# Row factors of a four-layer graph network: spread over the partitions by DMA instead of by TensorE

## What is computed

```
x = layernorm(x + L0(x, adj))      # attention, 4 heads of 32
x = layernorm(x + L1(x, adj))      # GAT, 1 head
x = layernorm(x + L2(x, adj))      # GAT, 8 heads of 16
x = layernorm(x + L3(x, adj))      # MLP, GAT of width 256 without mask, MLP, GAT of width 128
# a GAT:  e = leaky_relu(s1[:, None] + s2[None, :], 0.2), masked by adj
#         out = softmax(e, axis=-1) @ h
```

## Time and profile before

| | |
|---|---|
| median of 3 runs | 1170.52 us (1170.07 to 1173.26) |
| the profiled execution | 1170.96 us, its span 1169.1 us |
| mean granted TensorE clock | 0.976 |
| busy, PE / DVE / ACT / POOL | 1057.2 / 924.0 / 740.8 / 260.1 us |
| DMA | 12.97 MB, 9490 packets |

### The profile page before, as it was taken

How to read it: one execution, slowest core, us unless ns; L and a number is a source line. 1 busy time by engine, 2 the same in 40 slices (tenths; PEclk the granted TensorE clock), 3 DMA queues, 4 the chain that set the end, 5 groups by cost and what they waited for, 6 DMA issues and landing times. The chain is left out here.

```text
span 1169.1 us, 26405 instructions
## 1 busy us (share of the span) xinstructions
PE 1057.2 (90%) x9333; PEld 778.1 (67%) x9333; DVE 924.0 (79%) x2514; ACT 740.8 (63%) x1901; POOL 260.1 (22%) x381
## 2 busy tenths in 40 slices
PE   2898999999999999999999999999999999889763
PEld 1566667868676776768677776767677767476342
DVE  4458898898898988888897888888898897877432
ACT  1788577767666776777676666677676765343432
POOL 0011212222222122222213122222213122230211
PEclk9999999999999999999999999999999999899876
DMA  3000000000000000000000000000000000000000
GB/s 117 2 10 11 10 2 11 1 10 2 19 2 20 1 20 1 11 10 2 19 2 20 1 12 9 11 10 2 20 1 11 1 11 6 5 10 1 10 9 10
DMA packets 9490, 12.97 MB, mean 11 GB/s; under 512 B 2705, under 2 KB 5009, under 8 KB 9233
## 3 DMA queue, kind: packets, MB, share of 16 engines
q1 hardware_dynamic: 9360, 11.28, 3.0%
HBM read 7.08 MB, written 4.19 MB: 10 GB/s over the span
## 5 line engine op out<-in xcount | busy, mean ns | idle before, releaser
L1119 DVE SCALAR_TENSOR_TENSOR P<-bank,t2e,mask_t 128x512 f32<-128x512 f32 x512 | 347.4, 740 | 22.7 <-PE bank L561 22.7
L941 DVE CUSTOM_DVE_ANT_0 probs<-bank,mask_add 128x512 f32<-128x512 f32 x256 | 171.3, 679 | 26.0 <-PE bank L462 25.5
L703 ACT ACTIVATE probs<-probs,neg_max 128x512 f32<-128x512 f32 x256 | 183.0, 717 | 13.2 <-DVE neg_max L949 13.1
L713 ACT ACTIVATE probs_t<-bank 128x512 f32<-128x512 f32 x256 | 148.3, 598 | 56.6 <-PE bank L470 55.8
L470 PE MATMUL bank<-ident,probs 128*128 128x128 f32 x1024 | 143.9, 276 | 10.7 <-ACT probs L703 6.6
L470 PEld LDWEIGHTS bank<-ident,probs 128*128 128x128 f32 x1024 | 113.8, 141 | 34.0 <-issue 16.1
L612 PE MATMUL bank<-t,l_P 128*128 128x257 f32 x512 | 125.2, 392 | 9.4 <-DVE l_P L1051 9.3
L571 PE MATMUL bank<-P,GH 128*32 128x512 f32 x1024 | 120.6, 613 | 10.4 <-issue 5.2
L612 PEld LDWEIGHTS bank<-t,l_P 128*128 128x128 f32 x512 | 95.0, 194 | 36.5 <-DVE l_P L1051 17.2
L748 ACT ACTIVATE x<-x,shift_l,rstd_l 128x128 f32<-128x128 f32 x256 | 104.1, 486 | 16.3 <-POOL shift_l L1252 16.1
L571 PEld LDWEIGHTS bank<-P,GH 128*32 128x32 f32 x1024 | 31.3, 112 | 84.0 <-issue 76.5
(11 more groups left out here) (161 smaller groups left out, 1914.7 us busy)
## 6 DMA issues: line engine op xcount, KB each, us to landing
x_in<-in_x SPq DMA_DIRECT2D x16, 256.0 KB, 2.7
out<-x SPq DMA_DIRECT2D x16, 256.0 KB, 2.0
l_P<-in_adj SPq DMA_DIRECT2D x1, 1024.0 KB, 5.0
w_fc<-in_L_gnn_W_fc SPq DMA_DIRECT2D x1, 256.0 KB, 3.0
probs_t<-in_L_gnn_a_fc SPq DMA_DIRECT2D x1, 256.0 KB, 5.8
w_cat<-in_L_gnn_W SPq DMA_DIRECT2D x2, 64.0 KB, 2.8
w3a<-in_L_gnn_mlp_w SPq DMA_DIRECT2D x1, 128.0 KB, 3.1
w3b<-in_L_gnn_mlp_w SPq DMA_DIRECT2D x1, 128.0 KB, 2.9
```

Of the source, the lines that this page charges most:

```text
L703: act.activation(e, e, ACT.Exp, bias=neg_max[:, m:m + 1], scale=SCALE0, accum_out=g.of(den0)[:, m:m + 1])\
L713: act.activation(probs_t[c % 2][:, h, :, :].rearrange("p j n -> p (j n)"), ps("l0_t", g, m)[:, :], ACT.Copy)\
L941: dve.tensor_tensor_reduce(probs[c % 2][:, h, :], ps("l0_s", g, m)[:, :], mask_add[:, c, :], 1.0, -3.0e38, ALU.add, ALU.max, row_max[:, m: ...
L1119: last = dve.scalar_tensor_tensor(P2[:, h % GROUP2, j, :], ps("l2_s", g, h)[:, :], g.of(t2e)[:, j, h:h + 1], mask_t[:, j, :], ALU.max, ALU ...
```

## The change

The transposes l1_s, l3_s, l3b_s, l2_s and the products l0_rd go, with their uses of PSUM banks. Instead SP moves the factors. For each of them a first DMA (`*_rows`) writes the tile [128, heads, 4] to a line in DRAM, [heads, 128 p, 4 c], in pieces of 16 bytes. Once it has landed, a second DMA per head (`*_spread`; four of 32 partitions each in layer 0) reads the 2 KB line and writes it to all 128 partitions of one of seven row buffers [128, 128 p, 4 c]. Before it reuses a row buffer, SP waits until VectorE has read it. Per graph these are 5 writes to DRAM and 15 spreading DMAs (12 x 256 KB in all).

The row buffer holds the factors in the order (p, c), since the line does. VectorE reads it with a rearranged view, "q p c -> q c p": 128 elements with a step of four float32 words, four times. All its other operands stay as they were. P, the mask and the output keep their order.

On POOL the large instructions over [128, 4 x 128] are cut in pieces of 128 columns: `l0_bias`, `l1_y`, `scale`, `l2_scale` and `below_zero` issue 4 (8 for layer 3's 1024 columns) where they issued 1. All five order tables and the bank table are new.

```diff
-            def l2_s(g, h):
-                if h == 0:
-                    pe.wait_ge(*sig("exp2", g, 3))
-                ps = empty("l2_s", g, h)
-                for c in range(C):
-                    last = pe.transpose(ps[:, c * P:(c + 1) * P], g.of(R2)[:, h, c:c + 1].broadcast_to([P, P]), ident[:, :])
-                last.then_inc(filled("l2_s", g, h), 1)
...
+            def lay_out(n, column, made):
+                def f(g, k):
+                    sp.wait_ge(*made(g))
+                    if n == "l0" and g.has(2):
+                        sp.wait_ge(*sig("o0_made", g, 1, back=2))
+                    sp.dma_start(g.of(line[n]).rearrange("h p c -> p h c"), column(g)).then_inc(signal[n + "_rows"], 16)
+                return f
+
+            def free_row(stage, g, k):
+                r, _, last = row_use[stage, k, g.i]
+                if last:
+                    sp.wait_ge(*row_read(last[0], last[2], last[1]))
+                return rows[r], row_filled[r]
+
+            def spread(n):
+                def f(g, k):
+                    if k == 0:
+                        sp.wait_ge(*sig(n + "_rows", g, 16))
+                    to, done = free_row(n + "_spread", g, k)
+                    sp.dma_start(to[:, :, :].rearrange("q p c -> q (p c)"),
+                                 g.of(line[n])[k].rearrange("p c -> (p c)").rearrange("(o n) -> o n", o=1)
+                                 .broadcast_to([P, N_NODES])).then_inc(done, 16)
+                return f
...
             def l2_p(g, h):
-                dve.wait_ge(*wrote("l2_s", g, h))
+                dve.wait_ge(*spread_done("l2_spread", g, h))
...
                 for j in range(C):
-                    last = dve.scalar_tensor_tensor(P2[:, h % GROUP2, j, :], ps("l2_s", g, h)[:, :], g.of(t2e)[:, j, h:h + 1],
-                                                    mask_t[:, j, :], ALU.max, ALU.mult)
-                last.then_inc(emptied("l2_s", g, h), 1)
+                    last = dve.scalar_tensor_tensor(P2[:, h % GROUP2, j, :].rearrange("q (c p) -> q c p", c=C),
+                                                    row("l2_spread", g, h)[:, :, :].rearrange("q p c -> q c p"),
+                                                    g.of(t2e)[:, j, h:h + 1],
+                                                    mask_t[:, j, :].rearrange("q (c p) -> q c p", c=C), ALU.max, ALU.mult)
+                last.then_inc(signal["p2_made"], 1)
...
             def scale(n, t):
                 def f(g, k):
                     pool.wait_ge(*sig(n + "_b", g, 3))
-                    h = g.of(t)[:, :, 2:2 + D]
-                    pool.tensor_tensor(h, h, g.of(t)[:, :, D + 2:D + 3].broadcast_to([P, C, D]), ALU.mult)\
-                        .then_inc(signal[n + "_gh"], 1)
+                    for c in range(C):
+                        h = g.of(t)[:, c, 2:2 + D]
+                        last = pool.tensor_tensor(h, h, g.of(t)[:, c, D + 2:D + 3].broadcast_to([P, D]), ALU.mult)
+                    last.then_inc(signal[n + "_gh"], 1)
```

More of the change, by code:

```diff
@@ L195, in bank_uses, with row_uses @@
     return used
+def row_uses():
+    used, transfers, last, at = {}, [0] * ROWS, [None] * ROWS, 0
+    for name, g, k in turns("sp"):
+        if name.endswith("_spread"):
+            r = int(ROW_OF_USE[at])
+            at += 1
+            transfers[r] += HEADS0 if name == "l0_spread" else 1
+            used[name, k, g.i] = r, transfers[r], last[r]
+            last[r] = name, k, g
+    return used
 def build_program(nc, x, adj, w, out):
     use = bank_uses()
+    row_use = row_uses()
     with ExitStack() as ctx:
@@ L277, in build_program @@
         O2_t = sb("O2_t", [P, N_NODES])
+        rows = [sb(f"row{r}", [P, P, C]) for r in range(ROWS)]
         h3_t = sb("h3_t", [P, 2, N_NODES])
@@ L297, in build_program @@
         bank_read = [sem(f"bank_read{b}") for b in range(BANKS)]
+        row_filled = [sem(f"row_filled{r}") for r in range(ROWS)]
         x_loaded = [sem(f"x_loaded{q}") for q in range(2)]
@@ L307, in build_program @@
         for n in GATS:
-            for what, k in (("c4", 1), ("dd", 2), ("b", 3)):
+            for what, k in (("c4", 1), ("dd", 2), ("b", 3), ("p", 1)):
                 sem(f"{n}_{what}", k)
@@ L346, in empty, with row, spread_done, row_read @@
             return bank[b]
+        def row(stage, g, k=0):
+            return rows[row_use[stage, k, g.i][0]]
+        def spread_done(stage, g, k=0):
+            r, transfers, _ = row_use[stage, k, g.i]
+            return row_filled[r], 16 * transfers
+        def row_read(stage, g, k):
+            reader = {"l0_spread": "o0_made", "l1_spread": "l1_p", "l3_spread": "l3_p", "l3b_spread": "l3b_p",
+                      "l2_spread": "p2_made"}[stage]
+            return sig(reader, g, k + 1)
+        line = {n: [nc.dram_tensor(f"{n}_line{q}", [parts, P, C], F32, kind="Internal").ap() for q in range(2)]
+                for n, parts in (("l0", HEADS0), ("l1", 1), ("l2", HEADS2), ("l3", 1), ("l3b", 1))}
         x_v = x.rearrange("b (p c) d -> b p c d", c=C)
@@ L483, in l0_pv @@
                 last.then_inc(filled("l0_pv", g, c), 1)
-            def l0_rd(g, k):
-                pe.wait_ge(*sig("rden0_made", g, 1))
-                ps = empty("l0_rd", g)
-                for c in range(C):
-                    for h in range(HEADS0):
-                        m = HEADS0 * c + h
-                        last = pe.matmul(ps[DH0 * h:DH0 * (h + 1), c * P:(c + 1) * P],
-                                         rden0[:, m:m + 1].broadcast_to([P, DH0]), ident[:, :], start=True, stop=True)
-                last.then_inc(filled("l0_rd", g), 1)
             def l0_y(g, k):
-                pe.wait_ge(*took("l0_rd", g))
+                pe.wait_ge(*sig("o0_made", g, 1))
                 ps = empty("l0_y", g)
@@ L1260, in l1_y @@
                 y = g.of(x2)
-                pool.tensor_tensor(y[:, :, :], y[:, :, :], g.of(x1)[:, :, :], ALU.add).then_inc(signal["x2_made"], 1)
+                for c in range(C):
+                    last = pool.tensor_tensor(y[:, c, :], y[:, c, :], g.of(x1)[:, c, :], ALU.add)
+                last.then_inc(signal["x2_made"], 1)
             def scale(n, t):
@@ L1273, in f @@
                     ready(g)
-                    pool.tensor_scalar(e[:, :, :], v(g)[:, :, :], 0.0, None, ALU.min).then_inc(signal[n + "_min"], 1)
+                    for c in range(C):
+                        for q in range(0, e.shape[2], P):
+                            last = pool.tensor_scalar(e[:, c, q:q + P], v(g)[:, c, q:q + P], 0.0, None, ALU.min)
+                    last.then_inc(signal[n + "_min"], 1)
                 return f
```

302 lines of the change are left out of this document (160 added, 142 removed), and 10 rows, old and new, of the table STAGES.

## The result

The changed kernel takes 1413.66 us (median of 4 runs, 1410.89 to 1415.71), the kernel before 1170.32 us in the same series (1170.07 to 1173.26). The ratio is 1.207, with a 95% interval of 1.204 to 1.210. The prediction was 1353 us in a range of 1245 to 1455, slower: direction and mechanism hold, and the time is 61 us above the forecast. Most of this document is about where these 61 us lie, and about what TensorE's 117 us of removed work are worth.

What follows compares the result with a forecast made beforehand. PE bounds the kernel; DVE, with 229 + 6 - 6 + 60 = +289 us, becomes the bound. 1171 + 139 (12 steady graphs) + 43 (ends) = 1353 us, range 1245 to 1455.

Steps and rivals of the forecast that it cites:

- What bounds the kernel: Steady part: PE bound at 63.6 us per graph, DVE next at 56.7; after the change DVE bounds at 74.8.
- PE gets back 117 us: Spreading work removed from PE: 117.2 us in full, 7.3 per graph, leaving PE 56.3 us per graph.
- The source's step: VectorE's 640 weight instructions reading at a four-word step: 0.36 us more each, +229 us of DVE, bounds +164 and +246.
- rival C: VectorE's stepped reads cost more, 2.08 ns each: 341 us instead of 229, about 1460 us; chance 0.06 together with Rival B.
- l3_p: Layer 3's 64 single-source instructions on DVE, now reading SBUF: some 0.70 us instead of 0.79, -6 us.
- What DVE pays to POOL: DVE instructions with both sources in SBUF are stopped by POOL: +60 us, bounds 20 and 104 plus 40.
- DVE as full as PE was, 96.5%: Steady part: DVE's 74.8 us per graph at 96.5% busy give 77.5, 11.6 more, +139 us over 12 graphs.
- The ends, +43: Outside the steady part: four graphs' worth of added DVE work, +72 us, 60% of it taken, +43.
- Transfers in the steady part, nothing: Two DMAs in a row per layer, about 5.5 us, covered by DVE's work of two other graphs: nothing.
- Rival A: The step costs nothing on VectorE's two-source instructions: 1109 us, faster; chance 0.12.
- Rival B: Transfers show through SP's in-order queue, with a DMA releasing DVE's weight instructions: 1450 to 1650 us; chance 0.06 with rival C.
- Rival D: Whole kernel: gain and loss cancel at 1.2 ns per read, 1171 us; chance 0.02.

Runs made afterwards that it cites:

- e1: Kernel before, with l1_p, l3b_p and l2_p reading a constant SBUF tile at a step of four words instead of the PSUM bank: 1385.1 us.
- e3: Changed kernel with VectorE reading the row buffer contiguously, without the reordering, so factors reach the wrong nodes: 1201.3 us.
- e8: Changed kernel with contiguous reads, no first DMA (rows spread from a fixed input line) and POOL's divided instructions made harmless: 1110.7 us.
- e2: Kernel before, with l1_p, l3b_p and l2_p reading a constant SBUF tile without gaps instead of the PSUM bank: 1186.4 us.
- e7: Changed kernel with POOL's large instructions in one piece again, all else kept: 1419.7 us.
- e12: Changed kernel with contiguous reads and no first DMA (rows spread from a fixed input line), POOL's divided work left whole: 1169.0 us.
- e5: Changed kernel without the first DMA and the wait for it, row buffers spread from a fixed line of the input: 1385.8 us.
- e6: Changed kernel with POOL's divided instructions kept in number and place but working on one column or only filling a tile: 1392.5 us.
- e9: Changed kernel with 512 more identity transposes on TensorE, their result overwritten, and its bank claimed ahead of the wait for weights: 1422.7 us.
- e10: Changed kernel with P and mask_t in (p, c) order, so TensorE takes the step in its weight loads and l2_n's transposes: 1289.2 us.
- e4: Changed kernel with the line written as (c, p), the first DMA in 4-byte pieces, VectorE reading without a step: 1805.8 us.

## Why the prediction was right, and which terms were mis-sized

**What bounds the kernel**: right. VectorE took TensorE's place: before, PE was 97% busy in the periods, after, DVE is 91% busy, and e1 and e3 show that the step alone does it.

**PE gets back 117 us**: right as work, and worth nothing in the periods. e1 keeps the transposes and has after's period (78.57 against 78.14). In e8, where PE is nearly full again, the period is 6.2 us shorter than before, and by the bound above 4.3 of these or more are theirs, of the 7.3 that they took. I expected PE busy near 940 us and it is 1060.5: the page of after alone would not show the removal, since the remaining products last longer at the lower clock and behind VectorE's weights (e3 has the same products at 997.0).

**The source's step**: the central term, right. I took 1.74 ns per read, 0.36 us more per instruction, 1.02 us apart and 1.10 alone. Four in a row start (4.26 - 1.14) / 3 = 1.04 us apart, and one lasts 1.14 in the median (1.02 to 1.32):

```profile
L1178 DVE SCALAR_TENSOR_TENSOR P<-row,t2e,mask_t x512: 1019/1136/1316, 125.7 to 1285.0; 128x512 f32<-128x512 f32 x171
```

By busy time the 640 cost 552.0 + 71.8 + 71.6 - 347.4 - 44.1 - 46.1 = 258 us against 229 and a bound of 246; the pure step, after against e3, is 245 (695.4 against 357.6 + 47.1 + 45.6). The last number of the first sum is l3b_p's row before:

```profile
L1037 DVE SCALAR_TENSOR_TENSOR l3b_P<-bank,l3b_b,mask_t 128x512 f32<-128x512 f32 x64 | 46.1, 739 | 6.8 <-PE bank L527 5.3 <-issue 1.5
```

Per read, the full rate's 1.04 ns and the step's 0.75 (from the two runs of four) make 1.79 ns, the value of the second row I used. The rate that the two single-source rows gave held for a form with two sources. The Trainium skill, "Vector Engine (DVE) Microarchitecture Reference", section 5.2, gives 1.73 ns per column for one source that hops by 4 KiB at every element. The trace has 1.79 at a step of four words, within 4%. The same section of the Trainium skill's "Vector Engine (DVE) Microarchitecture Reference" has the 2.50 ns that rival C named for both sources, or the destination alone, at a step of 24 words. Here one source has the step, and no run shows the dearer case.

**l0_o** was 6 us as predicted (17.3 against 10.9). **l3_p** was not: I expected 0.70 us from L881's step, and it takes 0.751 where the contiguous form of e3 takes 0.541:

```profile
L1109 DVE TENSOR_SCALAR l_P<-row,l_g,l_b 128x512 f32<-128x512 f32 x64 | 33.8, 541 | 7.3 <-issue 4.0 <-DMA row<-l_line 3.3
```

The step costs this form 0.21 us, less than the 0.38 of the two-source form.

**What DVE pays to POOL**: wrong, and in its direction. I gave DVE +60 us. Sum up what is measured: 258 + 6 - 3 = 261, and DVE's total grew by 240.5, so all else on DVE fell by 20, 9 of them at L1102, which is L1161 in after:

```profile
L1102 DVE TENSOR_TENSOR small<-t,dmax_all 128x32 f32<-128x32 f32 x16 | 11.7, 733 | 0.1
```
```profile
L1161 DVE TENSOR_TENSOR small<-t,dmax_all 128x32 f32<-128x32 f32 x16 | 2.9, 181 | 0.1
```

The weights themselves pay 258 - 245 = 13 us for something else than the step, so the whole of it is about -7. Two steps failed. The size was too high even with POOL undivided: in e2, with contiguous reads from SBUF, DVE is busy 956.8 us, 33 more than before. And what I had said of the division, that it "changes how long one stop is, not their sum", does not hold: undivided (e7), DVE is busy 19 us longer. A quarter of the length stops a VectorE instruction for little (L1161 takes its 0.18 us undisturbed), while POOL, with 400 more instructions, is busy 184 us longer. Part of that is a fixed cost: 128 pieces e<-v at their shortest, 0.517 us, are 66 us against the 44.3 of 16 whole ones. The rest fits a wait between VectorE's instructions; a piece lasts 0.886 us in the median:

```profile
L1341 POOL TENSOR_SCALAR e<-v x128: 517/886/1482, 252.1 to 1367.7; 128x128 f32<-128x128 f32 x128
```

The Trainium skill, "SBUF — State Buffer", section "SBUF: two separate sides", has the pair of ports as an exclusive lock that goes to the one that starts first, for its whole instruction. The rows fit: a piece's 0.886 us are its 0.517 and a wait shorter than one weight instruction of 1.1 us. No row shows the lock itself.

**DVE as full as PE was, 96.5%**: wrong. It is 91%. The largest waits among its idle 76 us of the middle window are for layer 3b's transfer (the first row, see below) and for the normalisation's chain over ScalarE and POOL:

```profile
DVE l3b_P L1094 <- issue: 28.9, 10, 3.9
DVE x L1032 <- ACT x L803: 14.2, 10, 1.5
DVE stats_l L1042 <- POOL x L1324: 8.4, 9, 0.9
```

I had DVE's busy time 48 us too high (1213 against 1165) and its filling 5% too high. The two errors cancel: the forecast was 77.5 us per graph, and it is 78.1. A right period from two wrong factors is luck as much as method.

**The ends, +43**: this is the term that was mis-sized; they grew by 108, and by 96 in the prediction's own count of four graphs. I priced only VectorE's added work there (four graphs' worth, 72 us), and took 60% of it. The runs split the 108. The step is 71 by e3 and 76 by e1. VectorE is busy 381.3 us at the ends of after and 301.8 at those of e3, so of the 79 us that the step adds there some 90% lie on the path, where I took 60%; the likely reason is that at the ends one graph's chain counts and little covers it. The transfers are 16 (e3 to e12) to 18 (after to e5): the prediction priced one chain at 5.5 us and named it for the last graph, but put no number in the sum. POOL's work, whose pieces lie on the last graph's chain, is 6 (after to e6) to 11 (e12 to e8). A rest of 9 stays in e8, which has none of the three; its cause stays open. The chain of waits of after, at its end, shows the two new members between TensorE's products (start, us, what):

```profile
1382.19 1.39 DMA l3b_line<-l3b_R
1383.59 4.13 DMA row<-l3b_line
...
1388.85 3.17 DVE l3b_P L1094 x3
...
1400.27 1.51 POOL e L1341 x3
```

In the prediction's count 10 us of its miss lie in the periods (149 in place of 139) and 53 at the ends (96 in place of 43).

**Transfers in the steady part, nothing**: nearly right as time, (78.14 - 77.50) x 11 = 7 us, and wrong as a picture. The work of two other graphs does not cover layer 3b. In each of the 16 graphs of after, layer 3b's first weight instruction starts 0.08 to 0.10 us after its row has landed, and in each of the eleven periods VectorE stands still before it. One of them, in the timelines of SP and DVE; the row lands at 774.70:

```profile
768.68 0.32 SPq L449 DMA_DIRECT2D l3b_line<-l3b_R  x1
771.07 0.32 SPq L463 DMA_DIRECT2D row<-l3b_line  x1
774.78 1.15 DVE L1094 SCALAR_TENSOR_TENSOR l3b_P<-row,l3b_b,mask_t 128x512 f32<-128x512 f32 x1 [3.70 <-issue]
```

These waits add up to 28.9 us called `issue` and 3.2 called DMA, 32 of VectorE's 76 idle us. In e5, where the row is there early, they are gone and others stand in their place, so that only 7 us come back:

```profile
DVE dmax L1132 <- PE bank L606: 30.1, 10, 3.4
```

Without the step the same transfers cost (65.07 - 63.81) x 11 = 14 us in the periods, and with 4-byte pieces (99.67 - 65.07) x 11 = 381.

**Rival A**, 1109 us if the step were free: its condition was tried in e3, and the result was 1201. The rival's number is met by e8 (1110.7), which needs the transfers' dependence and POOL's work gone too. As priced, A was 92 us too optimistic: it let VectorE fill to 96.5% (84% in e3), put nothing for transfers and for POOL's waits, and took 10 us off the ends, which grew by 37 in e3. **Rival B** is not what bounds after, but its sign, a DMA that ends VectorE's waits, is there in layer 3b. **Rival D**, no change: no.

**The range's high end** had POOL at 110 us where its own bounds say 104 plus 40. With 144 the same working gives about 1480. The measured time lies inside either way.

**The clock**: I had written that it would add to the time only if PE's chain shows again. e9 fits this for the periods.

## What to carry to other kernels

- Before work goes from TensorE to a DMA, look at the order in which the DMA leaves the data, and at who then reads it with a step. Here each of the three places tried for the step was dear: on VectorE 212 us, on TensorE's weight loads 88 (e10 against e3), in the DMA's pieces 604 (e4 against e3).
- The gain of an engine that is relieved ends where the next one fills: with 117 us off TensorE, no run here came out more than 60 us below the kernel before, and that one leaves out part of the work. Cut a pipeline's time into start, period and end, and price each with its own chain; here work that was added to every graph counted almost in full at the ends.
- A wait that the profile calls `issue` can be a transfer. Compare the start of the instruction with the landing of what it reads.
- Dividing POOL's work moved the cost to POOL: 184 us more there, 19 us less on VectorE, and a total that stayed almost as it was.

## What the runs showed that I had not expected

- A two-source VectorE instruction with one source at a step of four float32 words: 0.38 us more per 512 elements (4.26 against 2.73 us for four in a row). With one source and two scalars (L1109): 0.751 against 0.541 us.
- TensorE's weight load of 128x128 float32 with the same step: 329 against 192 ns, and the products between them 397 against 275 ns.
- The first DMA with pieces of 4 bytes: 17.1 us to landing for 16 KB, against 3.6 with pieces of 16 bytes. The spread of a line of 2 KB to 128 partitions lands in 4.0 us, where a plain load of 256 KB takes 2.7.
- POOL's pieces of 128x128 between 0.52 and 1.48 us, and the tiny L1307 (128x4) at 1.18 us in the mean instead of 1.02. With the same POOL work it takes 1.49 in e1 and 1.20 in e2, so what VectorE does beside it matters.
- A mean granted clock of 0.92, a mix of 2.4 and 1.2 GHz, in periods in which TensorE is 80% busy, and 0.76 at the end, where it is 58% busy; before, 1.00 at 97% and 0.86 at 72%.
